# TensorE's value matmuls in a two-block Swin kernel, issued in four groups of two windows instead of eight groups of one

## What is computed

```python
y = layer_norm(x, ln1_g, ln1_b)
...
attn = jnp.einsum('whnd,whmd->whnm', q, k) * hd ** (-0.5)
...
attn = jax.nn.softmax(attn.reshape(-1, HEADS, N, N), axis=-1)
out = jnp.einsum('whnm,whmd->whnd', attn, v).transpose(0, 2, 1, 3).reshape(-1, N, Cc)
out = out @ proj_w + proj_b
...
x = x + out
z = layer_norm(x, ln2_g, ln2_b)
z = jax.nn.gelu(z @ fc1_w + fc1_b, approximate=False)
return x + (z @ fc2_w + fc2_b)
```

## Time and profile before

| | |
|---|---|
| runs | 1193.92, 1196.58 and 1200.53 us; median 1196.58 us |
| profiled execution, first to last instruction | 1195.6 us (its whole device time isn't listed apart) |
| TensorE busy | 1034.2 us (86%) |
| VectorE busy | 927.2 us (78%) |
| GpSimd busy | 523.4 us (44%) |
| ScalarE busy | 500.9 us (42%) |
| mean granted clock of TensorE | 0.922 of full speed |
| DMA | 8 GB/s over the span |

### The profile page before, as it was taken

How to read it: one execution, slowest core, us unless ns; L and a number is a source line. 1 busy time by engine, 2 the same in 40 slices (tenths; PEclk the granted TensorE clock), 3 DMA queues, 4 the chain that set the end, 5 groups by cost and what they waited for, 6 DMA issues and landing times. The chain is left out here.

```text
span 1195.6 us, 24594 instructions
## 1 busy us (share of the span) xinstructions
PE 1034.2 (86%) x8398; PEld 656.2 (55%) x8398; DVE 927.2 (78%) x1427; ACT 500.9 (42%) x1000; POOL 523.4 (44%) x830
## 2 busy tenths in 40 slices
PE   4888887888888878899978888888888879899978
PEld 3554555555555555455545555555555545555548
DVE  3669988888888885888779889887888885888513
ACT  2434444443444433455543445344444433455410
POOL 2134555444445551154464455544445542185500
PEclk9789999988889998899999999988999988999978
DMA  8000000000000000000000000000000000000003
GB/s 187 1 1 1 2 1 0 0 0 0 0 0 0 0 1 1 1 1 0 0 1 2 2 1 0 0 0 0 0 0 0 0 0 2 1 0 0 1 1 108
DMA packets 16833, 9.41 MB, mean 8 GB/s; under 512 B 14228, under 2 KB 16276, under 8 KB 16788
## 3 DMA queue, kind: packets, MB, share of 16 engines
q1 hardware_dynamic: 15776, 6.64, 2.5%
q10 hardware_dynamic: 1012, 2.16, 0.6%
HBM read 5.59 MB, written 3.21 MB: 7 GB/s over the span
## 5 line engine op out<-in xcount | busy, mean ns | idle before, releaser
L350 POOL TENSOR_TENSOR qexp<-qsb,conb 128x392 f32<-128x392 f32 x256 | 234.6, 949 | 52.1 <-ACT qsb L487 50.7
L999 PE MATMUL PS<-qexp,kbd 128*113 128x392 f32 x512 | 240.7, 554 | 6.9 <-issue 5.9
L362 POOL TENSOR_TENSOR osl<-osb,osh 128x392 fp32r<-128x392 f32 x64 | 79.9, 1248 | 368.5 <-ACT osh L525 368.5
L514 ACT ACTIVATE pt<-PS 113x392 f32<-113x392 f32 x256 | 126.8, 496 | 237.7 <-PE PS L999 237.2
L790 DVE TENSOR_SCALAR kexp<-ksb,conb 128x392 fp32r<-128x392 f32 x256 | 205.8, 875 | 9.7 <-ACT ksb L475 9.7
L795 DVE TENSOR_REDUCE nmax<-PS 98x8 f32<-98x392 f32 x256 | 141.0, 561 | 84.1 <-PE PS L999 83.7
L819 DVE RECIPROCAL rec<-PS 128x392 f32<-128x392 f32 x64 | 166.3, 2602 | 27.3 <-PE PS L999 26.4
L999 PE MATMUL PS<-kexp,qbd 128*98 128x392 f32 x256 | 104.9, 410 | 86.2 <-DVE kexp L790 79.2
L999 PE MATMUL PS<-bt,dup_r 113*113 113x392 f32 x256 | 176.3, 689 | 0.0
L999 PE MATMUL PS<-pt,vbd 113*32 113x49 f32 x4096 | 101.3, 219 | 18.4 <-ACT pt L514 9.6
L615 ACT ACTIVATE hid<-PS,vecb 128x392 f32<-128x392 f32 x128 | 75.2, 587 | 100.1 <-PE PS L999 94.7
(11 more groups left out here) (159 smaller groups left out, 1643.0 us busy)
## 6 DMA issues: line engine op xcount, KB each, us to landing
XW<-x_dram SPq DMA_DIRECT2D x14, 196.0 KB, 4.6
out_dram<-XW SPq DMA_DIRECT2D x14, 196.0 KB, 2.4
qexp<-w_dram ACTq DMA_DIRECT2D x2, 384.0 KB, 6.9
conb<-c_all_dram ACTq DMA_DIRECT2D x1, 656.5 KB, 4.4
hid<-c_sel_dram ACTq DMA_DIRECT2D x1, 512.0 KB, 8.1
qexp<-x_dram SPq DMA_DIRECT2D x2, 196.0 KB, 4.5
out_dram<-qexp SPq DMA_DIRECT2D x2, 196.0 KB, 2.4
conb<-c_all_dram ACTq DMA_DIRECT2D x1, 128.0 KB, 2.5
```

The costliest lines, as they stand in the source:

```text
L350: nc.gpsimd.tensor_tensor(qexp[buf][:, w, :, :], qsb[:, w * NTOK:(w + 1) * NTOK].rearrange("p (a n) -> p a n", a=1).to_broadcast([128, HEA ...
L362: nc.gpsimd.tensor_tensor(osl[:, :], osb[part][:, :], osh[:, :].bitcast(F32), ALU.subtract)\
L514: nc.scalar.activation(pt[w % 4][:, :], bST[w % 2][0:KROWS, 0:HEADS * NTOK], ACT.Exp)\
L999: return nc.tensor.matmul(o, a, b, start=start, stop=stop, **k)
```

## The change

Only the order of calls in TensorE's `step` changes; no instruction is added or removed, no wait is taken out, and the other engines' programs stay as they are. `pv(0)` moves behind `f_qk` and `scores_t(2)`, next to `pv(1)`. `scores_t(4)` moves ahead of `pv(2)`, and `pv(3)` moves up next to `pv(2)`, both ahead of `f_v`. `pv(4)` moves down and `pv(5)` up to stand together behind `scores_t(6)`, which itself moves ahead of `ahead(5)`. `pv(6)` and `pv(7)` already stood together at the end. (The file has also lost 25 empty lines at its top, so line 999 of before is line 974 of after.)

```diff
@@ -1112,10 +1087,10 @@
                 scores_t(p, blk, u, G, 1, u, f)
                 if not first:
                     den(G - 1, 1)
-                pv(G, 0, u, f)
                 if more:
                     f_qk(p, G + 1, nb)
                 scores_t(p, blk, u, G, 2, u, f)
+                pv(G, 0, u, f)
                 pv(G, 1, u, f)
                 scores_t(p, blk, u, G, 3, u, f)
                 if more2:
@@ -1130,27 +1105,27 @@
                     pe.wait_ge(res_done, G)
                 if tail:
                     tail[0]()
+                scores_t(p, blk, u, G, 4, u, f)
                 pv(G, 2, u, f)
+                pv(G, 3, u, f)
                 if more:
                     f_v(p, nb, range(WIN))
                 if tail:
                     tail[1]()
-                scores_t(p, blk, u, G, 4, u, f)
                 ahead(1)
-                pv(G, 3, u, f)
                 ahead(2)
                 scores_t(p, blk, u, G, 5, u, f)
                 ahead(3)
-                pv(G, 4, u, f)
                 if tail:
                     tail[2]()
                 ahead(4)
                 den(G, 0)
+                scores_t(p, blk, u, G, 6, u, f)
+                pv(G, 4, u, f)
+                pv(G, 5, u, f)
                 ahead(5)
-                scores_t(p, blk, u, G, 6, u, f)
                 ahead(6)
                 ahead(7)
-                pv(G, 5, u, f)
                 scores_t(p, blk, u, G, 7, u, f)
                 if more:
                     maxt(G + 1)
```

## The result

The changed kernel takes 1241.26 us (median of 4 runs, 1238.18 to 1244.34) against 1195.25 us for the kernel before (4 runs). It is slower: ratio 1.0369, 95% interval 1.0336 to 1.0402. The profiled execution has a span of 1242.5 us; it is the slowest of the four (1244.34 us).

What follows compares the result with a forecast made beforehand. It took a step to be a ring through VectorE and TensorE, where stalls between `ahead(0)` and `pv(7)` move the step's end. 1195.6 span + 39 waits + 4.5 clock + 1.0 to the median gave 1240 us, range 1213 to 1266.

Steps and rivals of the forecast that it cites:

- The ring and its cover: Step loop: VectorE 10.27 us, TensorE 11.73, closing 2.65; TensorE's work ahead of `ahead(0)` has 2.98 us of cover.
- The switch at 0.09 in and 0.09 out: TensorE entering and leaving small matmuls: 0.18 us a group; three pairs saved a half, 0.54 us, the first worth nothing.
- rival 4: Whole kernel faster by the switches alone: 0.54 us x 32 = 17 us, 1179 us; chance 0.03.
- Part one, the uncovered wait for PS5: Behind `f_v`, with `scores_t(4)` moved ahead: 1.38 us stall during ScalarE's `vbd` copies; `ahead(1)` 1.24 us later.
- `den(G,0)` 0.74 late: Middle of step: late `expo(4)` and `osb` delay `osh`, `osl` and `den(G,0)`, from 427.63 to 428.37.
- Part two: Behind `den(G,0)`, the late half: `ahead(7)` stalls 0.40 us, `maxt` at about 433.2 against 431.67, `pv(7)` 1.36 later.
- The sum of 1.3 us a step: Loss over both places in 30 steps: 39 us; bounds 0.67 to 1.7 us a step.
- The clock term of 4.5 us: TensorE's clock in the steps: one more slow stretch in every eighth step, 0.15 us a step, 4.5 us.
- rival 2: Clock gets worse: one more slow stretch in most steps, 37 us more, 1273 us (1254 to 1290); chance 0.15.

Runs made afterwards that it cites:

- experiment 6: Kernel before plus 12 additional matmuls ahead of `ahead(0)`, with only `pv(0)` next to `pv(1)` and `pv(3)` next to `pv(2)` ahead of `f_v`: 1158.08 us, ratio 0.9682.
- Experiment 3: Changed kernel with one of ScalarE's two copies of `vbd` left out, TensorE's order unchanged: 1223.61 us, ratio 1.0246.
- experiments 5 to 8: All with 12 additional matmuls: changed order 1203.97 us; early pairs only 1158.08; changed, `scores_t(4)` back behind `f_v`, 1165.70; changed, from `ahead(3)` on as before, 1196.89.
- experiments 2 and 8: Changed kernel with the order from `ahead(3)` on as before: 1233.94 us (2); the same with 12 additional matmuls ahead of `ahead(0)`: 1196.89 us (8).
- held clock: Condition of runs with 12 additional matmuls ahead of `ahead(0)`, in TensorE's wait for `kexp`; kernel before with them: 1165.51 us, clock 1.00 over eleven steps.
- experiment 4: Kernel before plus 12 additional matmuls (2.2 us at full clock) ahead of `ahead(0)`, in the wait for `kexp`: 1165.51 us, ratio 0.9742.
- experiment 5: Changed kernel plus 12 additional matmuls ahead of `ahead(0)`: 1203.97 us, ratio to the kernel before 1.0048.
- experiment 1: Changed kernel with only `scores_t(4)` put back behind `f_v`: 1213.85 us, ratio 1.0153.
- experiment 9: Kernel before with `scores_t(4)` and `pv(2)` moved ahead of `ahead(0)`, `pv(0)` next to `pv(1)`, no additional matmuls: 1175.31 and 1183.61 us; two other runs set aside.

## Why the prediction was right

It gave 1240 us, slower; measured were 1241.26. By its steps:

- **The ring and its cover**: right. `ahead(0)` starts 10.2 us after `den` in the changed kernel too, the wait for `kexp` is 3.30 us instead of 2.98, and experiment 6 fits a pair ahead of it that brings nothing.
- **The switch at 0.09 in and 0.09 out**: right, 0.18 us a step by experiment 6. As a forecast for the whole change (rival 4, 1179 us) the switches alone were off by 62 us, because they leave out what lies over which wait. The rule of the Trainium skill ("TensorEngine Tiling (Array Packing)", Key Properties), that a change of tiling mode drains TensorE, fits the 0.18 us; no run here tells a drain from another cost of the switch.
- **Part one, the uncovered wait for PS5**: right in mechanism and size. `ahead(1)` comes 4.54 us after `ahead(0)` (4.49 walked), the idle time is 1.31 (1.38), the wait occurs 30 times with 39.3 us (some 40). Experiment 3 shows that it is paid in full, experiments 5 to 8 that it costs 1.2 us a step. A remainder I had not seen: `scores_t(4)` now inherits the wait for the residual, which `pv(2)` used to carry; in the step shown it costs 0.02 us at most (0.20 from `bn` to `qexp`, plain distance 0.18).
- **`den(G,0)` 0.74 late**: mis-sized. It starts 7.25 us after `ahead(0)`, before 6.94: 0.31 late. ScalarE's copy `osb` was late nearly as walked (0.69), but GpSimd's `osl` took 1.24 us instead of 1.61 (below).
- **Part two**: the stalls are there (`ahead(7)` 1.26 us after `ahead(5)`, 1.12 walked; `maxt` 1.27 later), but its price is small: 0.1 us a step net of a switch saved. In the expectations of experiments 2 and 8 I gave the late half a larger share of the loss than it has, and was 14 and 7 us out at the near end; the two parts simply add.
- **The sum of 1.3 us a step**: somewhat too high. It was walked in a step of 24.65 us, and from such a step to the 25.91 after are 1.26. But at held clock the steps of the order of before alternate between 24.65 and 24.9, and the mean difference is 1.11 (25.89 against 24.77). 30 x 1.11 = 33 us of the 38.5. The rest lies outside these steps, and a part of it isn't the change. Of the 39.7 us between the two profiled executions (1202.8 and 1163.1), 3.1 stand ahead of TensorE's first `f_qk` (row `z,wk`, at 49.17 against 46.04), where the two orders are still the same and where the profiles of all these kernels lie anywhere between 45.9 and 49.2; 1.2 stand at the start of the second block, ahead of its first `f_v` in a step (21.63 against 20.45 us, at mean clocks of 0.69 and 0.92). The prediction had no term for either.
- **The clock term of 4.5 us**: the sign was right, the way was not. By the ratios the change costs 44.1 us free and 36.6 at held clock, so 7.5; by the medians, each over its own kernel before, 46.0 and 40.5, so 5.5. The two held runs are from different chips, so the size is uncertain. It was to come from one more slow stretch in every eighth step. In the eleven steps of the first block nothing of the kind is there: slow stretches cost 1.5 us a step in both orders (26.28 - 24.77, 27.37 - 25.89). In the profiles more than the whole term stands in the second block. Twelve steps before, twelve after:

```profile
638.62:950.28 311.66, 269.97 (x2708) 174.84 (x2700) 267.43 (x373) 137.29 (x277) 155.08 (x157) 0.93 0.00 0
```

```profile
659.32:996.23 336.91, 273.14 (x2702) 179.57 (x2702) 271.00 (x372) 135.95 (x277) 152.88 (x157) 0.89 0.00 0
```

At held clock the same twelve take 297.8 (experiment 4) and 311.0 us (experiment 5), so the clock costs 13.9 us before and 25.9 after. Three of the steps after took near 30.7 us at a mean clock of 0.78, which is rival 2 in three steps instead of thirty. This is one execution, and the slowest of the four.

The agreement to 1 us is partly luck, because errors cancel: the steps were put 5.6 us too high (39 against 33.4), the time outside them at nothing (5 to 7 us), the clock 1 to 3 us too low, and the sum started at 1196.6 us, 1.3 above the median of the four runs. What the prediction got right by its working is the way, and 33 of its 39 us.

What stays open: why the clock costs experiment 1 so much (1213.9 us free, 1165.7 held, 48 us, against 31 in the order of before). Its steps have more slow time (a mean clock of 0.90 in the loop against 0.92 and 0.94), but no run varied the length of the idle time alone, so what makes one order suffer more than another wasn't separated.

## What to carry to other kernels

Before closing a gap between two groups on an in-order engine, ask what the instruction between them covers: here a 0.18 us switch was saved, and a 1.2 us copy by another engine laid open, once per step. Find the next wait behind the moved piece, and put something ahead of it that is as long as the wait's cause. And if TensorE must idle for some microseconds in each round, filling the idle time, with real work first and with additional matmuls for the rest, can be worth more than the order of the real work: 1165.5 us against 1196.87 beside it, with nothing else changed.

## What the runs showed of the hardware

- Additional matmuls of 2.2 us in a 3.0 us wait held TensorE's granted clock at 1.00 over the steps of the loops and made the kernel 2.6% faster (experiment 4). With 1.98 us of the wait left idle (experiment 9) the clock of eleven steps was 0.94.
- GpSimd's `osl`, one and the same instruction, took 1.61 us for part 0 of a half and 1.02 for part 1 before, and 1.24 for part 0 in the changed kernel. VectorE's `lt<-lt,lv` ran wholly beside the first of these and took its plain 0.56 us. In the changed kernel it started later within `osl` and took 0.92. So beside each other the two take 2.17 and 2.16 us in sum, against 1.58 apart (1.02 and 0.56), and which of them pays is different in the two orders. That is read from rows that overlap; no run took one of the two instructions away. The rows: GpSimd and VectorE before, then GpSimd and VectorE after.

```profile
425.87 1.61 POOL L362 TENSOR_TENSOR osl<-osb,osh 128x392 fp32r<-128x392 f32 x1 [3.80 <-ACT osh L525]
433.91 1.02 POOL L362 TENSOR_TENSOR osl<-osb,osh 128x392 fp32r<-128x392 f32 x1 [6.43 <-ACT osh L525]
```

```profile
426.04 0.56 DVE L774 SCALAR_TENSOR_TENSOR lt<-lt,lv 128x392 f32<-128x392 f32 x1
```

```profile
795.34 1.24 POOL L337 TENSOR_TENSOR osl<-osb,osh 128x392 fp32r<-128x392 f32 x1 [4.48 <-ACT osh L500]
```

```profile
796.08 0.92 DVE L749 SCALAR_TENSOR_TENSOR lt<-lt,lv 128x392 f32<-128x392 f32 x1
```
